# The softmax scaling of batch 0 moves from VectorE to GpSimd, ahead of the clearing of buffers

## The chip, the core and the metric

The kernel runs on one core of one Trainium2 chip. The metric is the time of one execution on the device in microseconds (us); lower is better. All numbers below are in us unless marked ns. TensorE multiplies matrices, VectorE (DVE in the rows) and ScalarE (ACT) do elementwise work, GpSimd (POOL) does elementwise work and issues its own DMAs, SyncE (SP) issues DMAs.

## What is computed

One layer on x of shape (8, 512, 512): 8 batches of 512 tokens with 512 features, all in float32.

```
xn  = layernorm(x)
out = x + attention(xn) + mixture_of_experts(xn)

attention, for each batch, 16 heads of 32, one key/value head for all:
    s = q @ k.T                 # 512 x 512, causal: row i sees columns 0..i
    p = exp(s - max) / sum      # softmax over each row
    o = p @ v
mixture of experts: 32 experts, 8 picked per token out of 2 of 4 groups,
    and a shared two-layer part (512 -> 1024 -> 512) with relu squared
```

## The kernel before, in words

The program has three parts, each written out engine by engine and held together by semaphores alone. `front` (0 to about 115 us) does the layer norm and the first projections. `middle` (about 115 to 1080 us) runs the 8 batches. `experts` does the routed experts to the end. The change lies in the first batch of `middle` (batch 0, about 115 to 260 us).

**A slot.** `middle` goes through each batch in 18 slots; slot s works on head s and finishes head s - 1. On TensorE a slot is: scores of head s for the row blocks 3 and 2, the down projection of the shared part for slot s - 2, scores of blocks 1 and 0, the first transposes of head s - 1, in slots 5, 9, 13 and 17 the product with the values, the up projection `up` of slot s (12 matmuls), more transposes of head s - 1, in slots 0, 4 and 8 the query projection of the next four heads, and the last transposes. The causal mask makes a head's four row blocks 512, 384, 256 and 128 columns wide, 1280 columns in all.

**VectorE's part of a slot.** `mask_and_min(s, i)` (L1088, a custom instruction that reads the scores from PSUM and the mask from SBUF) for two blocks; `shared(s - 1)`: two tensor_tensor instructions of 256 columns, L1104 and L1108, whose inputs both lie in SBUF; `mask_and_min` for two more blocks; in batch 0 a piece of the routing of the experts (it picks experts for all tokens); at last `scale(s)`: a reciprocal of the row sums (L1094) and four tensor_scalar instructions (L1098) that multiply the four blocks of `m_sc` in place by it.

**The other engines.** ScalarE computes the exponentials (L934) between `mask_and_min` and the reciprocal, then, in its slot s, the relu of `up` (L968), and copies of the transposes. In batch 0 ScalarE also rounds the last 9 of 21 pieces of the weights (`high_piece`, L170), two in each of the slots 0 to 3 and one in slot 4, always behind the relu of that slot. GpSimd subtracts to get the low part of each piece (L244) as soon as its high part is there. Behind the last piece GpSimd fills `empty`, writes it over the tail of `slot_rows` in device memory (`clear_tail`, L418: 31 x 128 rows of 1156 bytes) and over the spare rows of `sums` (L841). Its next work, scattering token rows to their expert slots (L856), is paced by batch 1's exponentials.

**Buffers that bind the order.** `m_sc` holds two heads. `mask_and_min(s)` waits until head s - 2 is scaled, exponentiated and fully transposed. The first transposes of head h wait for its scaling and for a copy by ScalarE.

Of the kernel before, what the change touches and what calls it, by code (L numbers as in the profile page):

```python
# [5 lines left out]
F32 = mybir.dt.float32  # L6
# [3 lines left out]
ALU = mybir.AluOpType  # L10
# [4 lines left out]
P = 128  # L15
B, S, D = 8, 512, 512
T = B * S
TB = S // P
G = T // P
KC = D // P  # L20
NH, HD = 16, 32
# [18 lines left out]
BASE = 16  # L40
# [15 lines left out]
def at(i, per, n):  # L56

    return i * per + (BASE + n)
# [38 lines left out]
def front(nc, sems, x, consts, fc1g, xnt_hi, xnt_lo, xh, xlo, rows, cst, logits, spare, weights, load_bias):  # L97


    with ExitStack() as ctx:  # L100
# [36 lines left out]
        piece_hi_made, piece_lo_made = sem("f_piece_hi_made"), sem("f_piece_lo_made")  # L137

        def part(which, piece):

            name, n = piece
            return weights[name][which][:, n * PIECE:(n + 1) * PIECE]
# [57 lines left out]
        def act_program(act, steps):  # L200
# [37 lines left out]

            in_a_row(((0, root), (1, high), (2, latent), (1, high_pieces)), B, R, steps)

        def pool_program(pool):
            for k, piece in enumerate(PIECES):
                pool.wait_ge(piece_hi_made, k + 1)
                nc.gpsimd.tensor_tensor(part(3, piece), part(1, piece), part(2, piece).bitcast(F32), ALU.subtract).then_inc(piece_lo_made, 1)  # L244

        def pe_program(pe, steps):
            if steps == FRONT_STEPS:
# [26 lines left out]
        def dve_program(dve, steps):  # L274
# [50 lines left out]
            if steps == FRONT_STEPS:  # L325
# [4 lines left out]
        last = (B // R - 1, R - 1)  # L330
        ends = dict(halves=(lo_made, after(*last, KC, KC)), latents=(xl_made, after(*last, TB, TB)), logits=(lg_made, after(*last, TB, TB)),
                    consts=(cst_in, 16), pieces=piece_lo_made,
                    halves_saved=[(xnt_saved[u], stored(B // R - 1 - u, u)) for u in range(R)],
                    latents_saved=[(xl_saved[u], xl_stored(B // R - 1, u)) for u in range(R)])
        return sp_program, pool_program, act_program, dve_program, pe_program, high_piece, ends


SHIFT_BLOCK = 4
# [9 lines left out]
PIECES_A_SLOT = 2  # L348
PIECES_OF = [(sum(PIECES_A_GROUP[:n]), sum(PIECES_A_GROUP[:n + 1])) for n in range(B)]
# [293 lines left out]
SPC = [0, 128, 384, 768]  # L643
# [31 lines left out]
def middle(nc, sems, x, bproj, xnt_hi, xnt_lo, xh, xlo, rows, wq, wkv, wproj, wup, wdown, cst, slots_sb, pads_sb, empty, xs, sums, partial,  # L675
# [3 lines left out]
    with ExitStack() as ctx:  # L679
# [73 lines left out]
        all_sent, tables_saved = sem("m_all_sent"), sem("m_tables_saved")  # L753

        NQ = 3 * 16

        def stacked(b, c):

# [74 lines left out]
                                  (xh_in, 32 * (B - 1)), (xlo_in, 32 * (B - 1))):  # L833
                sp.wait_ge(landed, value)

        def pool_program(pool):

            pool.wait_ge(*early["consts"])
            routing.clear_tail(pool)
            for a in sums:  # L840
                pool.dma_start(a[T:T + SPARE, :], empty[:, 0:LAT]).then_inc(zeroed, 16)  # L841
            pool.wait_ge(routing.slots_made, 2)
            pool.wait_ge(routing.pads_made, 1)
            pool.wait_ge(routing.tagged_saved, 16)
            pool.wait_ge(routing.expert_saved, 64)
            pool.wait_ge(routing.tail_sent, 16)
            for sem_, value in early["latents_saved"]:
                pool.wait_ge(sem_, value)

            def load(g):  # L850
                pool.dma_start(row[g % 2][:, :], rows[g * P:(g + 1) * P, :]).then_inc(row_in[g % 2], 16)

            def scatter(g, k):
                pool.wait_ge(exp_done, BASE + NH * TB + (g * TOPK + k) * PACE // (2 * TOPK))
                pool.sem_inc(pool_passed, 1)
                pool.indirect_dma_start(out=xs, out_offset=bass.IndirectOffsetOnAxis(ap=slots_sb[:, g, k:k + 1], axis=0),  # L856
                                        in_=row[g % 2][:, :], in_offset=None).then_inc(sent[g % 2], 16)

            def fill(g):
                pool.indirect_dma_start(out=xs, out_offset=bass.IndirectOffsetOnAxis(ap=pads_sb[:, g:g + 1], axis=0),  # L860
                                        in_=empty[:, :], in_offset=None, bounds_check=SLOTS - 1,
                                        oob_is_err=False).then_inc(pads_sent, 16)

            load(0)
            for g in range(G):
                if g % 2 == 0:
                    for a in sums:
                        pool.dma_start(a[g * P:(g + 2) * P, :].rearrange("(g p) l -> p g l", p=P),
                                       empty[:, 0:LAT].unsqueeze(1).broadcast_to([P, 2, LAT])).then_inc(zeroed, 16)
                pool.wait_ge(row_in[g % 2], 16 * (g // 2 + 1))  # L870
                pool.sem_inc(pool_passed, 1)
                for k in range(TOPK):
                    scatter(g, k)
                    if k == TOPK // 2 - 1 and g + 1 < G:
                        if g >= 1:
                            pool.wait_ge(sent[(g + 1) % 2], 16 * TOPK * ((g + 1) // 2))
                        load(g + 1)
                fill(g)
            for u in range(2):
                pool.wait_ge(sent[u], 16 * TOPK * G // 2)  # L880
            pool.wait_ge(pads_sent, 16 * G)
            pool.wait_ge(zeroed, 16 * len(sums) * (1 + G // 2))
            pool.sem_inc(all_sent, 1)
# [138 lines left out]
        def dve_program(dve, last_logits):  # L1022
# [55 lines left out]
            def batch(b, first):  # L1078
                def mask_and_min(h, i):
                    k = h * TB + ROWS.index(i)  # L1080
                    dve.wait_ge(s_done, at(b, NH * TB, k + 1))
                    if i == ROWS[0]:
                        dve.wait_ge(t_done, at(b, 3 * NH, 3 * (h - 1)))
                        dve.wait_ge(exp_done, at(b, NH * TB, TB * (h - 1)))
                        dve.wait_ge(scaled, at(b, NH, h - 1))
                    n = (i + 1) * P
                    dve.sem_inc(dve_passed, 1)
                    nc.vector.tensor_tensor_reduce(out=sc[:, h % 2, SPC[i]:SPC[i] + n], in0=psS[k % 2][:, 0:n],  # L1088
                                                   in1=mask[:, S - n:S], scale=1.0, scalar=3.0e38, op0=ALU.add,
                                                   op1=ALU.min, accum_out=low[:, h % 2, i:i + 1]).then_inc(s_out, 1)  # L1090

                def scale(h):
                    dve.wait_ge(exp_done, at(b, NH * TB, TB * (h + 1)))
                    nc.vector.reciprocal(inv[:, h % 2, :], total[:, h % 2, :]).then_inc(inv_made, 1)  # L1094
                    dve.wait_ge(inv_made, at(b, NH, h + 1))
                    for i in range(TB):
                        cols = sc[:, h % 2, SPC[i]:SPC[i] + (i + 1) * P]
                        last = nc.vector.tensor_scalar(cols, cols, inv[:, h % 2, i:i + 1], None, ALU.mult)  # L1098
                    last.then_inc(scaled, 1)
# [105 lines left out]
        def pe_program(pe, last_multiply):  # L1205
# [52 lines left out]
            def batch(b, first):  # L1258
# [35 lines left out]

                def transposes(h, g):
                    if g == 0:
                        pe.wait_ge(scaled, at(b, NH, h + 1))
                        pe.wait_ge(ta_out, at(b, 2 * NH, 2 * h))
                        todo = [(0, 0, i) for i in range(4)]
                    elif g == 1:  # L1300
# [489 lines left out]
def build(nc, x, w_fc1_gate, gate_bias, wq, wkv, wproj, bproj, wup, wdown, w1, w2, wfc2, consts, out):  # L1790
# [10 lines left out]
    with ExitStack() as ctx:  # L1801
        cst = ctx.enter_context(nc.sbuf_tensor("cst", [P, NCONST], F32))
        sems = ctx.enter_context(ExitStack())
        with ExitStack() as inner:
# [22 lines left out]
            def load_bias(sp):  # L1827
                sp.dma_start(bia, gate_bias.partition_broadcast(P)).then_inc(bias_in, 16)

            *early, high_piece, front_ends = front(nc, sems, x, consts, w_fc1_gate, xnt_hi, xnt_lo, xh, xlo, rows, cst, logits,  # L1830
                  front_spare[:, :, :].rearrange("p c n -> p (c n)"), {n: (w, raw[n], *halves[n]) for n, w in named}, load_bias)
            attention = middle(nc, sems, x, bproj, xnt_hi, xnt_lo, xh, xlo, rows, halves["wq"], halves["wkv"], (proj_raw, proj_hi, proj_lo), halves["wup"], halves["wdown"],
                   cst, slots_sb, pads_sb, empty, slot_rows, sums, partial, logits, biased, picked, ot, bias_in, bia, experts_dram, shifts_dram, wproj, front_ends)
# [9 lines left out]
        @block.gpsimd  # L1843
        def _(pool):
            early[1](pool)
            attention[1](pool)
            late[1](pool)

        @block.scalar
# [65 lines left out]
```

## Time and profile before

| | |
|---|---|
| time, median of 3 runs | 1730.41 (1730.21 to 1731.7) |
| the profiled execution: its time, its span | 1730.02, 1728.2 |
| busy in the span: TensorE, VectorE, ScalarE, GpSimd | 1620.8, 1205.5, 1073.1, 821.0 |
| mean granted TensorE clock | 0.986 of full |

The span is what the profiler saw of the execution's instructions; 1.8 lie around it. Busy times of an engine are sums over its instructions, so an engine that waits in one stage and is full in another shows a mean that describes neither. The times of the rows below count from the start of the span.

### The profile page before, as it was taken

How to read it: one execution, taken by the hardware profiler on the slowest of the kernel's cores; microseconds unless marked ns; L12 is line 12 of the kernel's file. 1: busy time of each engine (PE TensorE's matmuls, PEld its weight loads, DVE VectorE, ACT ScalarE, POOL GpSimd, SP SyncE). 2: the span in 40 equal slices, each digit the busy share in tenths (PEclk: the TensorE clock that was granted, in tenths of full speed). 3: DMA queues.
4: the chain of work that ended last, by engine and by line, in shares of the span. 5: the costliest groups of instructions: out<-in, count | busy, mean ns of one | idle time of the engine just before them, and what ended most of it. 6: DMA issues, size and time to landing. Idle time of an engine off the chain costs nothing.

```text
span 1728.2 us, 40624 instructions
## 1 busy us (share of the span) xinstructions
PE 1620.8 (94%) x10811; PEld 1388.4 (80%) x10811; DVE 1205.5 (70%) x3669; ACT 1073.1 (62%) x2799; POOL 821.0 (48%) x669
## 2 busy tenths in 40 slices
PE   5887789999999999999999999899999999999999
PEld 5775667777777877777777777799999999999987
DVE  7779987777868777778687777355555555555567
ACT  3355565666757756757577577366666666666642
POOL 0213002434524524435344344277777877778760
PEclk9899899999999999999999999999999999999999
DMA  7953823434434334344344344599999999989794
GB/s 280 387 166 102 134 63 99 142 115 145 140 96 151 124 126 153 113 137 136 116 138 133 105 151 141 117 183 188 182 195 187 189 187 198 201 172 162 137 260 184
DMA packets 193091, 273.72 MB, mean 158 GB/s; under 512 B 37400, under 2 KB 133791, under 8 KB 190820
## 3 DMA queue, kind: packets, MB, share of 16 engines
q0 software_dynamic: 60352, 92.59, 24.8%
q1 hardware_dynamic: 77572, 113.01, 23.2%
q10 hardware_dynamic: 54944, 65.52, 12.8%
q8 instruction: 94, 1.54, 0.4%
q14 instruction: 129, 1.06, 0.2%
HBM read 121.83 MB, written 129.67 MB: 146 GB/s over the span
## 4 chain that ended last, share of the span: by engine, by line
PE 58%; DVE 18%; issue 10%; DMA 5%; POOL 4%; ACT 3%; DVEq 1%; SPq 1%; ACTq 0%; POOLq 0%
PE e_psH L1710 10%; PE e_psY L1721 10%; DVE m_sc L1088 5%; POOL sums L1675 4%; PE m_psO L1339 4%; PE m_psU L64 3%; PE m_psS L1292 3%; PE m_psT L1317 3%; PE m_psY L64 3%; PE m_psU L66 3%; PE m_psU L65 3%; DVE m_sc L1098 3%; PE m_psY L65 3%; PE m_psY L66 3%; PE e_psX L1695 3%
## 5 line engine op out<-in xcount | busy, mean ns | idle before, releaser
L1675 POOL DMA_INDIRECT sums<-e_y,e_where x287 | 445.9, 1554 | 153.4 <-issue 96.5
L856 POOL DMA_INDIRECT slot_rows<-m_row,slots x256 | 266.1, 1039 | 470.4 <-ACT m_sc L934 436.8
L934 ACT ACTIVATE m_sc<-m_sc,m_low 128x512 f32<-128x512 f32 (+3 forms) x512 | 283.7, 556 | 161.5 <-DVE m_low L1088 160.1
L1710 PE MATMUL e_psH<-e_xt,e_w_of 128*128 128x128 f32 x2296 | 305.1, 276 | 3.3 <-ACT e_xt L1570 3.3
L1721 PE MATMUL e_psY<-e_w,e_ht 128*128 x1148 | 295.7, 380 | 1.5 <-ACT e_ht L1581 1.5
L1088 DVE CUSTOM_DVE_ANT_0 m_sc<-m_psS,cst 128x512 f32<-128x512 f32 (+3 forms) x512 | 229.4, 485 | 83.1 <-PE m_psS L1292 82.5
L1710 PEld LDWEIGHTS e_psH<-e_xt,e_w_of 128*128 128x128 f32 x2296 | 280.5, 193 | 3.7 <-ACT e_xt L1570 3.5
L1576 ACT ACTIVATE e_w_of<-e_w 128x512 f32 x287 | 180.9, 630 | 118.1 <-issue 116.1
L1721 PEld LDWEIGHTS e_psY<-e_w,e_ht 128*128 128x128 f32 x1148 | 196.2, 191 | 17.2 <-issue 2.5
L1292 PE MATMUL m_psS<-m_ks,m_qs 96*128 96x256 f32 (+2 forms) x512 | 160.2, 372 | 52.1 <-DVE m_low L1088 45.1
L1631 DVE TENSOR_SCALAR e_where<-e_row,e_shifts 128x1 uint32<-128x1 uint32 x287 | 61.5, 214 | 196.5 <-DMA sums<-e_y,e_where 178.2
L1098 DVE TENSOR_SCALAR m_sc<-m_sc,m_inv 128x128 f32<-128x128 f32 (+3 forms) x512 | 173.0, 407 | 4.5
L1581 ACT ACTIVATE e_ht<-e_relu 128x256 f32<-128x256 f32 x287 | 119.6, 417 | 87.5 <-DVE e_relu L1618 86.2
L1292 PEld LDWEIGHTS m_psS<-m_ks,m_qs 96*128 96x128 f32 x512 | 88.3, 191 | 98.4 <-DVE m_low L1088 84.2
L1618 DVE TENSOR_SCALAR e_relu<-e_psH 128x256 f32<-128x256 f32 x287 | 121.7, 424 | 60.1 <-PE e_psH L1710 58.7
L1317 PE MATMUL m_psT<-cst,m_sc 128*128 128x128 f32 x1082 | 163.1, 277 | 0.2
L64 PE MATMUL m_psU<-xh,wup_lo 128*128 128x256 f32 x512 | 157.6, 308 | 0.0
L66 PE MATMUL m_psU<-xh,wup_hi 128*128 128x256 f32 x512 | 146.2, 286 | 0.0
L65 PE MATMUL m_psU<-xlo,wup_hi 128*128 128x256 f32 x512 | 146.1, 285 | 0.0
L1634 DVE TENSOR_SCALAR e_y<-e_psY,e_row 128x256 f32<-128x256 f32 x287 | 139.0, 484 | 1.9 <-issue 1.7
L1317 PEld LDWEIGHTS m_psT<-cst,m_sc 128*128 128x128 f32 x1082 | 126.8, 143 | 3.6 <-issue 2.2
L1695 PE MATMUL e_psX<-cst,e_row 128*128 128x128 f32 x574 | 109.6, 273 | 0.0
(233 smaller groups left out, 3228.2 us busy)
## 6 DMA issues: line engine op xcount, KB each, us to landing
e_row<-slot_rows ACTq DMA_DIRECT2D x287, 144.5 KB, 3.7
m_qs<-m_qhi SPq DMA_DIRECT2D x256, 64.0 KB
e_w<-in_w SPq DMA_DIRECT2D x256, 64.0 KB
f_xt<-in_x SPq DMA_DIRECT2D x8, 1024.0 KB, 11.4
m_qs<-m_qlo SPq DMA_DIRECT2D x128, 64.0 KB
m_res<-in_x SPq DMA_DIRECT2D x8, 1024.0 KB, 5.8
sums<-empty POOLq DMA_DIRECT2D x32, 256.0 KB
partial<-m_res ACTq DMA_DIRECT2D x16, 512.0 KB
```

The costliest lines, as they stand in the source:

```text
L64: pe.matmul(out, ll, rh, start=first, stop=False)
L65: pe.matmul(out, lh, rl, start=False, stop=False)
L66: return pe.matmul(out, lh, rh, start=False, stop=last)
L856: pool.indirect_dma_start(out=xs, out_offset=bass.IndirectOffsetOnAxis(ap=slots_sb[:, g, k:k + 1], axis=0), in_=row[g % 2][:, :], in_offse ...
L934: nc.scalar.activation(cols, cols, ACT.Exp, bias=low[:, h % 2, i:i + 1], scale=-1.0, accum_out=total[:, h % 2, i:i + 1]).then_inc(exp_done, 1)
L1088: nc.vector.tensor_tensor_reduce(out=sc[:, h % 2, SPC[i]:SPC[i] + n], in0=psS[k % 2][:, 0:n], in1=mask[:, S - n:S], scale=1.0, scalar=3.0e ...
L1098: last = nc.vector.tensor_scalar(cols, cols, inv[:, h % 2, i:i + 1], None, ALU.mult)
L1292: pe.matmul(psS[k % 2][:, 0:n], qs[:, (b * NH + h) % QR, i * P:(i + 1) * P], ks[:, 0:n], start=True, stop=True).then_inc(s_done, 1)
L1317: mm = pe.transpose((*psT, psO)[bank][:, to:to + P], sc[:, h % 2, SPC[i] + j * P:SPC[i] + (j + 1) * P], ident)
L1675: pool.indirect_dma_start(out=both_sums, out_offset=bass.IndirectOffsetOnAxis(ap=where[u % NY][:, 0:1], axis=0), in_=y[u % NY][:, :], in_o ...
L1710: mm = pe.matmul(psH[u % 2][:, k * P:(k + 1) * P], w1_of[u % 2][:, c * INTER + k * P:c * INTER + (k + 1) * P], xt[u % 2][:, c * P:(c + 1) ...
L1721: mm = pe.matmul(psY[u % 2][:, 0:LAT], ht[u % 2][:, c * P:(c + 1) * P], w_f[:, bass.ds(e * (2 * W) + (W + c * LAT), LAT)], start=(c == 0), ...
```

## The change

In batch 0 the four multiplications of each head are issued by GpSimd (`scale_first`) and signalled by a semaphore of their own, `scaled0`. VectorE returns from `scale` right behind the reciprocal. GpSimd's instruction has a second operation, a multiplication by 1.0. GpSimd's program is written by slots: first the low parts of the pieces that ScalarE rounds in that slot, then the scaling of that head. Clearing the tail and zeroing the spare rows of `sums` come behind head 15. Batches 1 to 7 are as before.

```
+        def low_piece(pool, k):
+            pool.wait_ge(piece_hi_made, k + 1)
+            nc.gpsimd.tensor_tensor(part(3, PIECES[k]), part(1, PIECES[k]), part(2, PIECES[k]).bitcast(F32),
+                                    ALU.subtract).then_inc(piece_lo_made, 1)
         def pool_program(pool):
-            for k, piece in enumerate(PIECES):
-                pool.wait_ge(piece_hi_made, k + 1)
-                nc.gpsimd.tensor_tensor(part(3, piece), part(1, piece), part(2, piece).bitcast(F32), ALU.subtract).then_inc(piece_lo_made, 1)
+            for k in range(PIECES_OF[-1][1]):
+                low_piece(pool, k)
...
+        def scaled_to(b, n):
+            return (scaled0, BASE + n) if b == 0 else (scaled, at(b - 1, NH, n))
...
-        def pool_program(pool):
+        def pool_program(pool, low_piece):
+            def scale_first(h):
+                pool.wait_ge(inv_made, at(0, NH, h + 1))
+                for i in range(TB):
+                    cols = sc[:, h % 2, SPC[i]:SPC[i] + (i + 1) * P]
+                    last = nc.gpsimd.tensor_scalar(cols, cols, inv[:, h % 2, i:i + 1], 1.0, ALU.mult, ALU.mult)
+                last.then_inc(scaled0, 1)
+
+            pool.sem_inc(scaled0, BASE)
+            for h in range(NH):
+                held = PIECES_OF[-1][1] + PIECES_A_SLOT * h
+                for k in range(held, min(held + PIECES_A_SLOT, len(PIECES))):
+                    low_piece(pool, k)
+                scale_first(h)
             pool.wait_ge(*early["consts"])
             routing.clear_tail(pool)
...
-                        dve.wait_ge(scaled, at(b, NH, h - 1))
+                        dve.wait_ge(*scaled_to(b, h - 1))
...
                     dve.wait_ge(inv_made, at(b, NH, h + 1))
+                    if first:
+                        return
                     for i in range(TB):
...
-                        pe.wait_ge(scaled, at(b, NH, h + 1))
+                        pe.wait_ge(*scaled_to(b, h + 1))
```

On VectorE, at the end of head 0 and the start of head 1, the order before was this (L1094 is the reciprocal, L1098 the scaling, L1088 `mask_and_min` of head 1, L1104 and L1108 the shared part):

```order
L1094 RECIPROCAL m_inv<-m_total 128x4
L1098 TENSOR_SCALAR m_sc<-m_sc,m_inv 128x128
L1098 TENSOR_SCALAR m_sc<-m_sc,m_inv 128x256
L1098 TENSOR_SCALAR m_sc<-m_sc,m_inv 128x384
L1098 TENSOR_SCALAR m_sc<-m_sc,m_inv 128x512
L1088 ISA m_sc,m_low<-m_psS,cst 128x512
L1088 ISA m_low 128x1
L1088 ISA m_sc,m_low<-m_psS,cst 128x384
L1088 ISA m_low 128x1
L1104 TENSOR_TENSOR m_sq<-m_relu 128x256
L1108 TENSOR_TENSOR m_sq_parts<-m_sq,m_sq_parts 128x256
```

In the changed kernel the same place on VectorE reads (its line numbers are some 22 higher):

```order
L1116 RECIPROCAL m_inv<-m_total 128x4
L1110 ISA m_sc,m_low<-m_psS,cst 128x512
L1110 ISA m_low 128x1
L1110 ISA m_sc,m_low<-m_psS,cst 128x384
L1110 ISA m_low 128x1
L1128 TENSOR_TENSOR m_sq<-m_relu 128x256
L1132 TENSOR_TENSOR m_sq_parts<-m_sq,m_sq_parts 128x256
```

The four multiplications are gone from VectorE, and head 1's masking follows the reciprocal. On GpSimd the pieces of slots 1 to 4 and what followed them stood in one row before, with no other work between them:

```order
L244 TENSOR_TENSOR wdown_lo<-wdown_raw,wdown_hi 128x512
L244 TENSOR_TENSOR wq_lo<-wq_raw,wq_hi 128x512
L244 TENSOR_TENSOR wdown_lo<-wdown_raw,wdown_hi 128x512
L414 MEMSET empty 128x289
L416 CAST empty<-cst 128x1
L418 DMA slot_rows<-empty 128x31x289
L841 DMA sums<-empty 128x256 x2
```

In the changed kernel the same pieces (those of slots 3 and 4) stand between scalings, one head's four after each slot's pieces (the waits are printed):

```order
L851 TENSOR_SCALAR m_sc<-m_sc,m_inv 128x512
L243 TENSOR_TENSOR wdown_lo<-wdown_raw,wdown_hi 128x512 [waits f_piece_hi_made]
L243 TENSOR_TENSOR wq_lo<-wq_raw,wq_hi 128x512 [waits f_piece_hi_made]
L851 TENSOR_SCALAR m_sc<-m_sc,m_inv 128x128 [waits m_inv_made]
L851 TENSOR_SCALAR m_sc<-m_sc,m_inv 128x256
L851 TENSOR_SCALAR m_sc<-m_sc,m_inv 128x384
L851 TENSOR_SCALAR m_sc<-m_sc,m_inv 128x512
L243 TENSOR_TENSOR wdown_lo<-wdown_raw,wdown_hi 128x512 [waits f_piece_hi_made]
L851 TENSOR_SCALAR m_sc<-m_sc,m_inv 128x128 [waits m_inv_made]
```

A head's scaling now waits on GpSimd for that slot's pieces, and the clearing (L414 to L841 before) has moved behind the last of 64 multiplications.

## Rows read from the trace of the kernel before

**Rows 1.** Stretches of batch 0, then batch 1; column heads first.
```profile
core 0: us, PE busy (x) PEld busy (x) DVE busy (x) ACT busy (x) POOL busy (x), PEclk, DMA share, GB/s
115.00:250.00 135.00, 103.64 (x617) 84.57 (x616) 126.23 (x466) 78.89 (x221) 16.75 (x14) 0.90 0.43 91
278.00:371.00 93.00, 89.25 (x618) 73.86 (x617) 72.89 (x252) 69.36 (x206) 43.90 (x47) 1.00 0.40 130
```

**Rows 2.** The same view for line 1094 alone, the reciprocal that ends each head.
```profile
122.00:251.00 129.00, 2.83 (x16) 0.89 0.42 86
278.50:371.00 92.50, 2.77 (x16) 1.00 0.40 130
```

**Rows 3.** The same view for line 1098 alone, the scaling on VectorE.
```profile
122.00:253.00 131.00, 25.82 (x64) 0.88 0.42 86
278.50:373.00 94.50, 20.91 (x64) 1.00 0.41 130
```

**Rows 4.** Who waited for whom, 120 to 240 us: total, times, longest.
```profile
PEld m_psS L1292 <- DVE m_low L1088: 29.7, 20, 4.6
```

**Rows 5.** Timeline of VectorE around the end of head 10: start, duration.
```profile
216.27 1.28 DVE L1098 TENSOR_SCALAR m_sc<-m_sc,m_inv 128x128 f32<-128x128 f32 x4
217.46 0.69 DVE L1059 TENSOR_TENSOR m_qlo<-m_q,m_qhi 128x512 fp32r<-128x512 f32 x1
218.06 0.69 DVE L1088 CUSTOM_DVE_ANT_0 m_sc<-m_psS,cst 128x512 f32<-128x512 f32 x1
219.15 0.43 DVE L1104 TENSOR_TENSOR m_sq<-m_relu 128x256 f32<-128x256 f32 x1
219.61 0.42 DVE L1108 TENSOR_TENSOR m_sq_parts<-m_sq,m_sq_parts 128x256 fp32r<-128x256 f32 x1
```

**Rows 6.** Timelines of GpSimd and VectorE where their work meets, slots 2 and 4.
```profile
142.07 1.30 POOL L244 TENSOR_TENSOR wdown_lo<-wdown_raw,wdown_hi 128x512 fp32r<-128x512 f32 x1 [7.48 <-ACT wdown_hi L170]
143.32 1.27 POOL L244 TENSOR_TENSOR wup_lo<-wup_raw,wup_hi 128x512 fp32r<-128x512 f32 x1
142.46 3.00 DVE L1098 TENSOR_SCALAR m_sc<-m_sc,m_inv 128x128 f32<-128x128 f32 x4
...
153.85 1.46 POOL L244 TENSOR_TENSOR wq_lo<-wq_raw,wq_hi 128x512 fp32r<-128x512 f32 x1
154.20 1.40 DVE L1108 TENSOR_TENSOR m_sq_parts<-m_sq,m_sq_parts 128x256 fp32r<-128x256 f32 x1
```

**Rows 7.** Timeline of GpSimd: its instructions with two, no and one input.
```profile
54.27 1.26 POOL L244 TENSOR_TENSOR wkv_lo<-wkv_raw,wkv_hi 128x512 fp32r<-128x512 f32 x1 [53.82 <-ACT wkv_hi L170]
160.82 0.33 POOL L414 MEMSET empty<- 128x289 f32 x1
161.22 0.18 POOL L416 CAST empty<-cst 128x1 uint32<-128x1 f32 x1
```

**Rows 8.** Timelines of GpSimd, TensorE, ScalarE, VectorE, batch 0, heads 0 to 5.
```profile
123.07 1.26 POOL L244 TENSOR_TENSOR wup_lo<-wup_raw,wup_hi 128x512 fp32r<-128x512 f32 x1
137.12 1.05 PE L1317 MATMUL m_psT<-cst,m_sc 128*128 128x128 f32 x4
141.38 0.61 ACT L170 ACTIVATE wdown_hi<-wdown_raw 128x512 fp32r<-128x512 f32 x1
154.10 0.60 PE L1317 MATMUL m_psT<-cst,m_sc 128*128 128x128 f32 x4
160.85 0.65 PE L1292 MATMUL m_psS<-m_ks,m_qs 96*128 96x512 f32 x2
163.98 0.67 DVE L1088 CUSTOM_DVE_ANT_0 m_sc<-m_psS,cst 128x512 f32<-128x512 f32 x1
```

**Rows 9.** The cleared tail: its issue, its landing; TensorE behind batch 0.
```profile
161.72 2.11 POOL L418 DMA_DIRECT2D slot_rows<-empty  x1 [0.32 <-POOL empty L416]
...
slot_rows<-empty POOLq DMA_DIRECT2D x1, 4479.5 KB, 19.8
...
260.80 0.47 PE L64 MATMUL m_psS<-xh,wq_lo 128*128 128x512 f32 x1 [1.48 <-DMA xlo<-xnt_lo]
```

More of the change, by code:

```diff
@@ L334, in front @@
                     latents_saved=[(xl_saved[u], xl_stored(B // R - 1, u)) for u in range(R)])
-        return sp_program, pool_program, act_program, dve_program, pe_program, high_piece, ends
+        return sp_program, pool_program, act_program, dve_program, pe_program, high_piece, low_piece, ends
 SHIFT_BLOCK = 4
@@ L755, in middle @@
         NQ = 3 * 16
+        scaled0 = sem("m_scaled0")
+        def scaled_to(b, n):
+            return (scaled0, BASE + n) if b == 0 else (scaled, at(b - 1, NH, n))
         def stacked(b, c):
@@ L1828, in load_bias @@
                 sp.dma_start(bia, gate_bias.partition_broadcast(P)).then_inc(bias_in, 16)
-            *early, high_piece, front_ends = front(nc, sems, x, consts, w_fc1_gate, xnt_hi, xnt_lo, xh, xlo, rows, cst, logits,
+            *early, high_piece, low_piece, front_ends = front(nc, sems, x, consts, w_fc1_gate, xnt_hi, xnt_lo, xh, xlo, rows, cst, logits,
                   front_spare[:, :, :].rearrange("p c n -> p (c n)"), {n: (w, raw[n], *halves[n]) for n, w in named}, load_bias)
@@ L1845, in _ @@
             early[1](pool)
-            attention[1](pool)
+            attention[1](pool, low_piece)
             late[1](pool)
```

## The prediction, made before the changed kernel ran

> **What bounds the kernel now.** I first read the busy time by stretch and looked for where batch 0 differs from a later batch. In 135 us of batch 0 VectorE is busy 126.2 and TensorE 103.6; in 93 us of batch 1 TensorE is busy 89.3 and VectorE 72.9 [rows 1]. From the first head's reciprocal to the last one's, 15 heads on, batch 0 takes some 129 us and batch 1 some 92.5 [rows 2]. Batch 0 is paced by VectorE, which carries the routing beside its usual work, and the later batches by TensorE. The waits say the same from the other side: in batch 0 TensorE's loads of the scores' weights waited 29.7 for VectorE's masking [rows 4]. What is saved in batch 0 reaches the end, since every batch after it is queued behind it on TensorE. VectorE spent 25.8 on 64 scaling instructions in batch 0, against 20.9 for the same 64 in batch 1 [rows 3]; the 4.9 on top is where they met GpSimd's work (below).
>
> **What GpSimd's scaling costs.** The trace has no tensor_scalar on GpSimd, so its price X for one head (four instructions, 1280 columns) has to be bounded. A one-column cast took 0.18, which I take as the fixed part, 0.72 for four. A subtraction with two inputs and 512 columns took 1.26 [rows 7], so (1.26 - 0.18) / 512 = 2.11 ns for each column, and X is at most 0.72 + 2.70 = 3.4. A memset with no input took 0.33 for 289 columns, (0.33 - 0.18) / 289 = 0.52 ns, and X is at least 0.72 + 0.66 = 1.4. The scaling reads one tensor where the subtraction reads two. I take half of the subtraction's price for a column, 1.05 ns, and X = 0.72 + 1.35 = 2.1. The second operation of the instruction may add to that; I have no row for it and leave it to the upper bound.
>
> **What VectorE gains in a slot.** The block of four scalings stood 1.19 before the next instruction (217.46 - 216.27) [rows 5]. Taken out, masking follows the reciprocal. But now GpSimd works on the same head just then. What such a meeting does stands in the trace: beside a GpSimd subtraction that began at 153.85, VectorE's L1108, which has two inputs in SBUF, took 1.40 [rows 6] in place of 0.42 [rows 5]; and the four scalings took 3.00 beside two subtractions [rows 6] in place of 1.28 [rows 5]. An instruction of this kind waited out the other engine's instruction. After the change the two maskings (1.09 from 218.06 to 219.15 [rows 5], with the mask alone in SBUF) should pass, and L1104 and L1108 come behind them. With X = 2.1 GpSimd's instructions last 0.32, 0.45, 0.59 and 0.72 and start some 0.3 after the reciprocal, so that L1104 finds the third under way (0.4 to wait) and L1108 the fourth (0.7). That is 1.1 of the 1.19 given back in each slot in which VectorE sets the pace. In slots where VectorE waits for TensorE before masking, the two don't meet.
>
> The Trainium skill (SBUF — State Buffer, Who interferes with whom) says that a VectorE instruction with two SBUF inputs and a GpSimd instruction that reads SBUF exclude each other for the whole instruction. The 1.40 row agrees. By this rule a slot is worth 0.1; if the engines only shared bandwidth it would be worth near 1.2, and the whole change 5 more.
>
> **The ring in slots 0 to 4.** This is the term I expect to decide. GpSimd must do the low parts of slot h before it scales head h. Those wait for ScalarE's high parts, which stand behind the relu of `up(h)`; `up(h)` stands on TensorE behind the first transposes of head h - 1; and these now wait for GpSimd's scaling of head h - 1. So the scaling of one head hangs on that of the head before through three engines. Before, this was no ring, since VectorE did the scaling. Its length without scaling: head 1's transposes began at 137.12 and the second piece of slot 2 ended at 143.32 + 1.27 = 144.59, 7.5 later, with ScalarE's first high part at 141.38 in between [rows 6, 8]. With X and two handovers of 0.1 each it is 7.5 + 2.1 + 0.2 = 9.8. The granted clock of TensorE was 0.90 in this stretch against 1.00 in batch 1 [rows 1]; I leave the 7.5 as it is.
>
> The ring starts when slot 0's pieces end at 123.07 + 1.26 = 124.3 [rows 8]: scaling of head 0 ends at 124.3 + 2.1 + 0.4 (a meeting with VectorE) = 126.8, transposes of head 1 begin at 126.8 + 9.8 + 0.1 = 136.7 (before 137.12), of head 2 at 146.5, of head 3 at 156.3, where before it was 154.10: 2.2 late. The scores of head 5 follow these by 160.85 - 154.10 = 6.75 [rows 8], at 163.1, and VectorE masks them at 163.4. Before, it came to them at 163.98 only, though they stood ready from 161.5 (160.85 + 0.65) [rows 8]. So VectorE's saving in five heads, which could have been 1.19 x 5 + 4.9 = 10.9, shrinks to **+0.6**.
>
> **Heads 5 to 15.** I count slots 5, 6, 7, 11 and 12 as paced by VectorE (their routing work leaves no idle time in front of the reciprocal): 5 x (1.19 - 1.1) = **+0.5**. In 8 to 10 and 13 to 15 VectorE already waits for TensorE at times; there the saving reaches TensorE only as earlier scores. Between 0 and 6 x 1.19 = 7.1 I take **+1.5**, near the lower end, because TensorE's transposes now wait for a scaling that ends X + 0.3 behind the reciprocal and not 1.2.
>
> **The moved clearing.** GpSimd issued it at 161.72 in 2.11, and 4479.5 KB landed after 19.8 [rows 9]. Under slots 5 to 7 nothing waited for it. It moves behind head 15's scaling, with the two stores of `sums`, ahead of GpSimd's first scatters. There it lies beside SyncE's load of batch 1's second half and the stacking of its queries, and TensorE already waited 1.48 for that load at 260.80 [rows 9]. What is behind it on GpSimd, the scatters, is paced by batch 1's exponentials and spread over seven batches, so that 20 late costs nothing. The load is sent before the clearing's packets begin; the stacked queries are sent in the middle of them. Between 0 and 3 (a share of the 19.8 that a 64 KB move could lose) I take **-1.0**. What it frees in slot 4, where it held VectorE, is in the 4.9 above.
>
> **Sum.** 0.6 + 0.5 + 1.5 - 1.0 = 1.6 faster: the profiled execution's 1730.0 goes to 1728.4, and the median, 0.4 above it, to **1728.8**. A measurement of this kernel can tell about 0.2% (3.5 us) from no change, so this is no change. Its own range, 1725 to 1733, is X from 1.8 to 2.6: each 0.1 of X costs 0.4 in the ring and 0.3 to 0.6 in the five locked slots.
>
> **Rivals.**
> *Scaling is cheap on GpSimd.* With X = 1.4 the ring is 9.1 and stays within VectorE's own pace, and the four instructions (0.25 to 0.47) are nearly over before L1104: 1.0 a slot is kept. 0.6 + 2.8 + 5.0 + 1.5 - 1.0 = 8.9, so 1721. For it: one input, and the memset's rate. Against: the subtraction's rate is four times the memset's, and there are two operations. The skill's GPSIMD Engine Reference, Engine selection, calls one-input work on GpSimd roughly line-rate, which would be an estimate of X near 1.8; no row here shows it. 18%.
> *It works as meant.* No ring, no lock: VectorE loses 25.8 of work; six slots paced by TensorE keep 7 of it. 19 faster, 1711. For it: VectorE's 94% in batch 0. Against: the 1.40 and 3.00 rows, and the queue order on GpSimd. 8%.
> *The ring sets the pace, slower.* One mechanism: slots 0 to 4 run at 7.5 + X + 0.2. The gain of 1.6 is gone from X = 2.3 on. At X = 3.4 the ring is 11.1, its end 4 x 1.3 = 5.2 later, and the same X lengthens the locks by 0.7 in five slots and TensorE's wait for scaling by 1 in all: 0.6 - 5.2 - 3.5 - 1.0 - 1.0 = 10 slower, 1740. Range 1733 to 1746. For it: two operations and software on GpSimd. Against: nothing in the trace but the one input. 32%.
> The forecast has 42%.
>
> **Chances.** Faster by over 0.2% (below 1727): 18 + 8 + 12 of the forecast's 42 = 38%. Within 0.2%: 28%. Slower (above 1733.9): 32 + 2 = 34%. The range reaches from inside the cheap case to the upper bound of X: 1718 to 1741, with some 9% out on either side.
>
> **What would show it.** In the changed profile GpSimd's 64 multiplications give X at once. The ring is right if the pieces of slots 1 to 4 on GpSimd are some 9.8 apart and TensorE waits for GpSimd in front of its transposes. The lock is right if L1104 and L1108's counterparts (L1128, L1132) in slots 5 to 7 take over 0.42. The reciprocals of heads 0, 5 and 15, 129 us from first to last before [rows 2], split the ring from what follows. The clearing is right if batch 1's first scores start no more than 3 later against batch 0's last reciprocal. The prediction is wrong if X is outside 1.8 to 2.6, or if TensorE, less often idle, is granted a full clock throughout batch 0: that would shorten the ring.

## The result: 0.3% slower, and the profile after

The changed kernel took 1736.09 us (median of 8 runs, 1732.4 to 1741.9), the kernel before 1730.34 beside it (8 runs, 1727.59 to 1734.22): 1.0031 of its time, 95% interval 1.002 to 1.0042, or 5.75 us slower by the medians. The ratios here and below are computed from the fast runs and not from the two medians, and differ from the medians' quotient by up to 0.0006. The profiled execution took 1737.02 with a span of 1735.2. The first lines of its page, with the busy time of each engine:

```profile
span 1735.2 us, 40635 instructions
## 1 busy us (share of the span) xinstructions
PE 1624.7 (94%) x10811; PEld 1389.9 (80%) x10811; DVE 1190.2 (69%) x3605; ACT 1073.8 (62%) x2799; POOL 864.6 (50%) x733
```

VectorE was relieved (1205.5 to 1190.2) and GpSimd loaded (821.0 to 864.6), as the diff says. The stretch of batch 0 that [rows 1] show, in the changed kernel:

```profile
core 0: us, PE busy (x) PEld busy (x) DVE busy (x) ACT busy (x) POOL busy (x), PEclk, DMA share, GB/s
115.00:250.00 135.00, 104.57 (x607) 84.54 (x607) 107.38 (x399) 77.43 (x217) 49.87 (x68) 0.86 0.28 53
```

VectorE fell from 126.2 to 107.4 in the same 135 us, and yet TensorE did no more work in them (607 instructions for 617) and was granted less clock, 0.86 for 0.90. VectorE is no longer the bound here, and something else is. The reciprocals split where the time went. All are us behind head 0's reciprocal, from the profiled executions:

```
              head 5    head 15   first of batch 1
before         50.08    128.77    156.55
after          53.52    131.72    162.20
```

So heads 0 to 5 lost 3.4, heads 5 to 15 won 0.5, and the stretch behind head 15 lost 2.7: 5.6 in all, near the 5.75 of the medians. That the two agree so well is partly luck, for the spans of the two profiled executions differ by 7.0. The changed one stood 1.2 earlier at head 0's reciprocal and took 2.6 more behind batch 1's first one (1452.2 for 1449.6), where the change touches nothing but when GpSimd's first stores start. The same remainder is 1451.3 to 1459.1 in the profiles of the experiments below, so nothing ties it to one part of the change.

**The ring.** GpSimd's timeline for slots 0 to 4 of the changed kernel (the row of a scaling is its block of four; in brackets how long the engine stood idle, and for whom):

```profile
121.92 1.27 POOL L243 TENSOR_TENSOR wup_lo<-wup_raw,wup_hi 128x512 fp32r<-128x512 f32 x1
123.17 2.81 POOL L851 TENSOR_SCALAR m_sc<-m_sc,m_inv 128x128 f32<-128x128 f32 x4
131.09 1.29 POOL L243 TENSOR_TENSOR wdown_lo<-wdown_raw,wdown_hi 128x512 fp32r<-128x512 f32 x1 [5.11 <-ACT wdown_hi L170]
132.34 1.45 POOL L243 TENSOR_TENSOR wup_lo<-wup_raw,wup_hi 128x512 fp32r<-128x512 f32 x1
133.77 3.61 POOL L851 TENSOR_SCALAR m_sc<-m_sc,m_inv 128x128 f32<-128x128 f32 x4
142.58 1.29 POOL L243 TENSOR_TENSOR wdown_lo<-wdown_raw,wdown_hi 128x512 fp32r<-128x512 f32 x1 [5.21 <-ACT wdown_hi L170]
143.82 1.73 POOL L243 TENSOR_TENSOR wup_lo<-wup_raw,wup_hi 128x512 fp32r<-128x512 f32 x1
145.53 2.55 POOL L851 TENSOR_SCALAR m_sc<-m_sc,m_inv 128x128 f32<-128x128 f32 x4
...
152.94 1.45 POOL L243 TENSOR_TENSOR wq_lo<-wq_raw,wq_hi 128x512 fp32r<-128x512 f32 x1
154.37 3.09 POOL L851 TENSOR_SCALAR m_sc<-m_sc,m_inv 128x128 f32<-128x128 f32 x4
...
163.91 2.06 POOL L851 TENSOR_SCALAR m_sc<-m_sc,m_inv 128x128 f32<-128x128 f32 x4
```

The first idle of each slot ends with ScalarE's high part, never with a reciprocal; the scaling follows the pieces without a gap. On TensorE the same slots show the other side, the first transposes of heads 0 to 3, and the scores of head 5:

```profile
126.04 1.12 PE L1341 MATMUL m_psT<-cst,m_sc 128*128 128x128 f32 x4 [3.03 <-POOL m_sc L851]
...
137.43 1.12 PE L1341 MATMUL m_psT<-cst,m_sc 128*128 128x128 f32 x4 [4.96 <-POOL m_sc L851]
...
148.13 0.66 PE L1341 MATMUL m_psT<-cst,m_sc 128*128 128x128 f32 x4 [2.19 <-POOL m_sc L851]
...
157.51 1.12 PE L1341 MATMUL m_psT<-cst,m_sc 128*128 128x128 f32 x4 [4.61 <-POOL m_sc L851]
...
165.56 0.65 PE L1316 MATMUL m_psS<-m_ks,m_qs 96*128 96x512 f32 x2
```

The turns are 11.4, 10.7 and 9.4 long. Four transposes took 1.12 behind the waits of 3.0, 5.0 and 4.6, and 0.66 behind the one of 2.2. VectorE in slots 3 and 5 of the same kernel:

```profile
152.37 0.90 DVE L1128 TENSOR_TENSOR m_sq<-m_relu 128x256 f32<-128x256 f32 x1
153.30 1.38 DVE L1132 TENSOR_TENSOR m_sq_parts<-m_sq,m_sq_parts 128x256 fp32r<-128x256 f32 x1
...
166.21 0.69 DVE L1110 CUSTOM_DVE_ANT_0 m_sc<-m_psS,cst 128x512 f32<-128x512 f32 x1 [5.24 <-PE m_psS L1316]
...
167.76 0.42 DVE L1132 TENSOR_TENSOR m_sq_parts<-m_sq,m_sq_parts 128x256 fp32r<-128x256 f32 x1
```

VectorE, once the bound, stood idle 5.24 for head 5's scores; before, they waited for it. The waits of 120 to 250 us, in total, number and longest. TensorE's wait for the masking, the last of them, was 32.6 in this window before (29.7 up to 240 us, [rows 4]):

```profile
PEld m_psT L1341 <- POOL m_sc L851: 18.2, 8, 5.2
DVE m_sc L1110 <- PE m_psS L1316: 17.2, 8, 5.2
...
PEld m_psS L1316 <- DVE m_low L1110: 14.9, 17, 4.1
```

**The clearing.** GpSimd behind head 15's scaling, which answers to [rows 9]:

```profile
257.10 2.00 POOL L422 DMA_DIRECT2D slot_rows<-empty  x1 [0.32 <-POOL empty L420]
259.11 1.15 POOL L863 DMA_DIRECT2D sums<-empty  x2
275.74 0.54 POOL L873 DMA_DIRECT2D m_row<-rows  x1 [15.48 <-DMA slot_rows<-empty]
```

and TensorE at batch 1's first scores, with the granted clock in the stretch that begins there and in an equal one behind it:

```profile
276.29 1.12 PE L1316 MATMUL m_psS<-m_ks,m_qs 96*128 96x512 f32 x2 [3.02 <-DMA m_qs<-m_qlo]
```

```profile
276.20:279.70 3.50, 3.41 (x9) 2.78 (x10) 1.18 (x4) 1.41 (x4) 1.54 (x3) 0.52 0.98 321
280.00:283.40 3.40, 3.40 (x23) 3.07 (x22) 1.57 (x7) 1.35 (x6) 2.06 (x2) 1.00 0.43 154
```

TensorE waited 3.02 for the stacked queries, which SyncE had sent while the clearing's packets were under way (the low parts at 270.84; the clearing, issued at 257.10, landed 17.9 later), and then worked for 3.4 us at half clock (1.2 GHz).

### The profile page after: what moved, and what is told of

Same layout as the page of the kernel before. It is cut to its first block, busy times and chain, and to the rows that moved or that the text cites. A ratio compares the mean times of both kernels' runs of the same rounds, so it can differ in the third digit from the quotient of the medians.

```text
span 1735.2 us, 40635 instructions
## 1 busy us (share of the span) xinstructions
PE 1624.7 (94%) x10811; PEld 1389.9 (80%) x10811; DVE 1190.2 (69%) x3605; ACT 1073.8 (62%) x2799; POOL 864.6 (50%) x733
## 3 DMA queue, kind: packets, MB, share of 16 engines
q14 instruction: 128, 1.05, 0.2%
## 4 chain that ended last, share of the span: by engine, by line
PE 67%; DVE 15%; issue 7%; DMA 4%; ACT 4%; POOL 2%; SPq 1%; DVEq 1%; ACTq 0%; POOLq 0%
PE e_psH L1734 14%; PE e_psY L1745 14%; DVE m_sc L1110 5%; PE m_psO L1363 4%; PE m_psU L64 4%; PE m_psT L1341 4%; PE e_psX L1719 4%; PE m_psU L66 3%; PE m_psU L65 3%; PE m_psS L1316 3%; PE m_psY L64 3%; PE m_psY L65 3%; PE m_psY L66 3%; DVE m_sc L1122 2%; ACT m_sc L956 2%
## 5 line engine op out<-in xcount | busy, mean ns | idle before, releaser
L1122 DVE TENSOR_SCALAR m_sc<-m_sc,m_inv 128x128 f32<-128x128 f32 x448 | 147.3, 399 | 4.0
```

## The experiments

Each was timed against the kernel before on its own chip (1730.48, 1730.45 and 1731.52 there). "Head 5" and so on are the marks of the table above. A mark is read from one execution, which can lie 3 us or more from the median of its kernel. So a mark tells where a time goes, and the median how much it is. Two pairs of profiles show how far a mark scatters. Up to head 5 the first experiment has the program of the changed kernel, and head 5 stood at 52.2 in it and at 53.5 there. The second has that of the kernel before, with 48.9 and 50.1.

**The clearing, alone.** From the changed kernel, the clearing goes back early, behind head 4's scaling:

```
                 scale_first(h)
+                if h == 4:
+                    pool.wait_ge(*early["consts"])
+                    routing.clear_tail(pool)
+                    for a in sums:
+                        pool.dma_start(a[T:T + SPARE, :], empty[:, 0:LAT]).then_inc(zeroed, 16)
-            pool.wait_ge(*early["consts"])
-            routing.clear_tail(pool)
-            for a in sums:
-                pool.dma_start(a[T:T + SPARE, :], empty[:, 0:LAT]).then_inc(zeroed, 16)
```

> The changed kernel with one part undone: GpSimd clears the tail and zeroes the spare rows behind head 4's scaling, about where it did before, and not behind head 15's. Theory 'the late clearing delays the stacked queries': batch 1's first scores no longer wait (3.0 us) for the DMA of the stacked queries, the stretch from head 15's reciprocal to the first one of batch 1 falls from 30.5 to about 27.8 us, and the time from about 1736 to about 1733.3. Rival 'the stretch is longer for another reason (ScalarE or TensorE behind it, a granted clock at half)': it stays near 30.5 and the time near 1736.

It took 1733.15 (1.0018, 1.0001 to 1.0034), 2.7 above the kernel before where the changed kernel is 5.75 above it; the intervals of the two overlap, and it is the mark that shows the place. Head 15 to batch 1's first reciprocal was 26.6, where the changed kernel has 30.5; the wait for the stacked queries was gone, and the clock there stayed at 1.00. The opposite, late clearing in the kernel before, with nothing else changed:

```
             pool.wait_ge(*early["consts"])
+            pool.wait_ge(t_done, at(0, 3 * NH, 3 * (NH - 1) + 1))
             routing.clear_tail(pool)
```

> The kernel before with one part of the change alone: VectorE scales as ever, but GpSimd's clearing waits for the first transposes of head 15. Theory 'the late clearing delays the stacked queries': heads 0 to 15 as before (128.8 us from first to last reciprocal), the stretch behind them 30 to 31 us in place of 27.8, the time about 1733. Rival 'the clearing is free there': 27.8 and 1730.4. With the scaling on VectorE the heads 0 to 15 tell nothing of it in either theory.

It took 1737.25 (1.0045, 1.0025 to 1.0064), 4 more than expected and no less than the changed kernel itself. The last stretch went from 27.8 to 32.3, and TensorE waited in it like this, in that kernel's trace:

```profile
272.50 1.12 PE L1293 MATMUL m_psS<-m_ks,m_qs 96*128 96x512 f32 x2 [4.25 <-DMA m_qs<-m_qlo]
```

So moving the clearing costs 3.9 and 4.5 us by the marks, 3.1 and 6.8 by the medians, scaling on GpSimd or not. In all six profiles with the late clearing TensorE waited for the stacked queries (3.0 to 4.3), and the 3.5 us behind the wait ran at 0.50 to 0.61 of the clock. In none of the others did it wait for them.

**The ring, cut.** In the changed kernel each head is scaled first, and the pieces of its slot come behind it:

```
             for h in range(NH):
+                scale_first(h)
                 held = PIECES_OF[-1][1] + PIECES_A_SLOT * h
                 for k in range(held, min(held + PIECES_A_SLOT, len(PIECES))):
                     low_piece(pool, k)
-                scale_first(h)
```

> The changed kernel, but in each slot GpSimd scales the head first and makes the low parts of the slot's pieces behind it. Theory 'ring': the scaling of head h no longer hangs on the up projection of its own slot; TensorE's waits for GpSimd in front of the transposes (16 us in batch 0) fall below 5, the first five heads fall from 53.5 us to 50 or less, and the time from about 1736 to 1730 to 1732. Rival 'lock only': what costs is VectorE and GpSimd meeting, which goes on; the five heads stay at 52 to 54 us and the time at 1735 or more.

It took 1731.58 (1.0004, 0.9992 to 1.0016), no longer slower than the kernel before, though the clearing is still late in it. Head 5's reciprocal stood at 46.6, 7.0 earlier than in the changed kernel and 3.5 earlier than before. Two lines changed places, and the first half of batch 0 went from a loss to a gain. The other way to leave the ring is to leave heads 0 to 4 to VectorE:

```
-                scale_first(h)
+                if h >= 5:
+                    scale_first(h)
...
-                    if first:
+                    if first and (h >= 5):
                         return
...
-                    last.then_inc(scaled, 1)
+                    last.then_inc(scaled0 if first else scaled, 1)
```

> The changed kernel, but VectorE still scales heads 0 to 4 and GpSimd heads 5 to 15; the clearing stays behind head 15. Theory 'ring plus lock': the first five heads take 50.1 us as in the kernel before; from head 5 to head 15 it takes 78 us, as in the changed kernel (78.2) and hardly less than before (78.7), since the lock and the later transposes eat the 1.2 us a slot; with 2.7 lost in the clearing the time is 1732 to 1733. Rival 'from head 5 on the move works as meant and only the ring spoils it': 70 to 73 us from head 5 to 15 and a time of 1725 to 1727.

It took 1733.08 (1.0009, 0.9995 to 1.0022): head 5 at 50.2 as before, heads 5 to 15 in 75.7 (before 78.7), the last stretch 30.7. With the early clearing as well:

> VectorE scales heads 0 to 4, GpSimd heads 5 to 15, and GpSimd clears the tail behind the last piece, about where it did before. No ring and no late clearing: the sum of what e1 and e4 showed. First five heads 50.2 us, heads 5 to 15 76 us, the stretch behind them 26.7 to 27.8: batch 1 starts 153 to 154 us behind head 0's reciprocal (156.6 before), and the time is 1727 to 1728. Rival 'the clearing in slot 5 costs what it did not cost at the end': 156 or more and 1730.

1728.73 (0.9989, 0.9974 to 1.0004), the last stretch 26.6. Heads 5 to 15 took 78.1 in this profile, though but for the clearing the program there is that of the 75.7. Most of the difference is in one slot, head 14's. It took 10.8 in four profiles (the changed kernel and the experiments so far with the clearing early, the pieces behind, and this one), and in all four TensorE's clock was 0.62 or 0.63 from 3 us before head 13's reciprocal to 1 behind it. In the profile of the 75.7, and in the three below that scale all heads with two operations and no extra work, it was 1.00, and the slot took 9.2 to 9.7. A gain of 0.5 or of 3 in this stretch thus comes with the clock of one execution and not with the program. Up to head 13 the scatter is small: heads 5 to 13 took 64.5 before and 61.9 to 63.3 in all these versions.

**Both repairs.** Pieces behind the scaling, clearing behind head 4:

> All 16 heads on GpSimd, each slot's pieces behind its scaling, the clearing behind head 4's scaling. The sum of what e1 and e3 showed: first five heads 46.6 us, heads 5 to 15 77.3, the stretch behind them 26.7 to 27.8; batch 1 starts 150.6 to 151.7 us behind head 0's reciprocal against 156.6 before, and the time is 1724.5 to 1726. Rival 'batch 0 is bound elsewhere, and what is saved in the first heads is given back': 154 or more and a time within 2 us of before.

1724.85 (0.9971, 0.9959 to 0.9984): faster than both kernels, 5.6 less than before. Its marks are 46.2, 121.9 and 148.3. That profiled execution took 1721.96, the lowest of its 12 runs, so the marks promise more than the median gives. The first scalings and first transposes, in its trace:

```profile
120.83 2.22 POOL L851 TENSOR_SCALAR m_sc<-m_sc,m_inv 128x128 f32<-128x128 f32 x4 [22.93 <-DVE m_inv L1117]
...
130.86 2.21 POOL L851 TENSOR_SCALAR m_sc<-m_sc,m_inv 128x128 f32<-128x128 f32 x4 [4.71 <-DVE m_inv L1117]
```

```profile
133.13 0.66 PE L1342 MATMUL m_psT<-cst,m_sc 128*128 128x128 f32 x4 [0.54 <-POOL m_sc L851]
...
142.62 0.66 PE L1342 MATMUL m_psT<-cst,m_sc 128*128 128x128 f32 x4 [0.53 <-POOL m_sc L851]
```

The scaling waits for the reciprocal now, and TensorE for the scaling only 0.54. Of all waits of this kernel from 119 to 255 us these two carry the comparison with the 18.2 and 14.9 above:

```profile
PEld m_psS L1317 <- DVE m_low L1111: 23.3, 22, 5.5
PEld m_psT L1342 <- POOL m_sc L851: 8.6, 11, 1.6
```

VectorE sets the pace again, with less to do.

**Is it a ring? More work in it.** Four small multiplications ahead of each head's scaling on GpSimd, into a buffer that nothing reads, once in the changed kernel and once in the version with both repairs:

```
+                for n in range(0, 16, 4):
+                    nc.gpsimd.tensor_scalar(spare_cols[:, h % 2, n:n + 4], mask[:, n:n + 4],
+                                            inv[:, h % 2, 0:1], 1.0, ALU.mult, ALU.mult)
```

> The changed kernel with four small GpSimd multiplications (4 columns, into a tile of their own that nobody reads) in front of each head's scaling, some 0.2 us each, 0.8 a head. Theory 'ring': in slots 0 to 4 GpSimd's time is on the path once a slot, so that the first five heads grow from 53.5 by four times 0.8, to about 56.7 us, and the time by 3 us or more, to 1739 to 1742. Rival 'GpSimd's length does not set the first heads' pace': 53 to 54.5 us there.

> The same four small multiplications in e7, where the pieces stand behind the scaling and there is no ring. Theory 'ring': 0.8 more a head is mostly hidden in the first five heads (46.2 to at most 47.5 us), and the time is 1725 to 1728. Rival: if GpSimd's length is on the path without the pieces in front as well, the first five heads grow by 3 us, as in e11.

They cost about 1.3 a head (64 of them 21.1 us) and not the 0.8 expected. In the changed kernel it took 1744.79 (1.0077, 1.0058 to 1.0095): the first transposes of heads 0 to 3 were 13.5, 11.8 and 12.0 apart, 5.8 more in three turns, and head 5 stood 6.3 later. With both repairs it took 1730.04 (0.999, 0.9977 to 1.0003), head 5 2.1 later. The same work costs three times as much in heads 0 to 5 where the pieces stand ahead of it. It is not free in the other version either, where both marks and time are above what was expected: TensorE waits up to 2.2 there for the scaling in place of 0.54. Over the whole kernel the work costs 7.5 us in the first and 4.1 in the second, by the medians against the kernel before beside each.

**The lock.** VectorE's two instructions with two SBUF inputs (L1128, L1132) come behind the last two maskings of their slot in batch 0:

```
-                    if 1 <= s <= NH:
+                    if 1 <= s <= NH and not first:
                         shared(s - 1)
...
                         mask_and_min(s, ROWS[3])
+                    if 1 <= s <= NH and first:
+                        shared(s - 1)
```

> The changed kernel, but in batch 0 VectorE does all four maskings before the two instructions of the shared part (L1128, L1132), so that they come some 0.7 us later, when GpSimd's scaling is mostly over. Theory 'lock': their busy time in batch 0, 19.4 us in the changed kernel against 14.5 before, falls toward 14; if the lock sets the pace in the slots with much routing, heads 5 to 15 fall from 78.2 to 76 us or less and the time by 2 to 3 us, to about 1733. Rival 'the lock is paid where VectorE has time': the busy time falls but heads 5 to 15 stay at 77.5 to 78.5 and the time stays at 1736; the first five heads may move either way, since the other instructions with two inputs still meet GpSimd's pieces.

1738.68 (1.0051, 1.0035 to 1.0067), no faster than the changed kernel. First how long the two were in the changed kernel, batch 0 and then batch 1, where GpSimd doesn't scale (the columns are the stretch, its length, VectorE's busy time in L1128 alone, the granted clock, the DMA share and GB/s; the second fence is the same for L1132):

```profile
119.00:256.00 137.00, 8.88 (x16) 0.85 0.26 49
278.00:375.00 97.00, 6.28 (x15) 0.99 0.41 136
```

```profile
119.00:256.00 137.00, 10.50 (x16) 0.85 0.26 49
278.00:375.00 97.00, 6.37 (x15) 0.99 0.41 136
```

Free they are 6.7 and 6.8 for 16, so meetings cost 2.2 + 3.7 = 5.9, or 0.37 a slot. In the kernel before they took 14.5 together in batch 0, so 4.9 of the 19.4 came with the change. In the experiment they took 7.61 and 7.59, so 4.2 was taken away, and still head 5 stood at 53.4 as in the changed kernel. Heads 5 to 15 took 75.7, as the theory of the lock had it, but 1.2 of those 2.5 are head 14's slot at full clock, and the last stretch took 32.8 for 30.5. Why the first heads won nothing is seen in slot 1, on GpSimd and on VectorE:

```profile
134.35 4.29 POOL L851 TENSOR_SCALAR m_sc<-m_sc,m_inv 128x128 f32<-128x128 f32 x4
```

```profile
135.80 0.77 DVE L1068 TENSOR_TENSOR m_q<-m_q,m_rot 128x512 f32<-128x512 f32 x1
136.49 0.68 DVE L488 TENSOR_TENSOR ot<-proj_raw 128x512 f32<-128x512 f32 x1
137.09 0.98 DVE L489 TENSOR_TENSOR ot<-proj_raw 128x512 f32<-128x512 f32 x1
```

The scaling met L1128 and L1132 at its start (134.01 to 135.16) and then the two-input instructions of the rotation and the routing, and took 4.29. In the changed kernel it had met the rotation and the routing too, and took 3.61. The same edit on the version with both repairs:

> e7 with the later shared part of e5. If the lock matters, 1 to 3 us less than e7 (1722 to 1725), heads 5 to 15 in 75 to 76 us; if it is paid where VectorE has time, the same as e7 within 1 us.

1726.66 (0.998, 0.9967 to 0.9992), 1.8 more than without it, with intervals that overlap; batch 1's first reciprocal stood 2.4 later. The 1 to 3 us that the lock should have given did not come.

**The second operation.** In the version with both repairs, one operation in place of two:

```
-                    last = nc.gpsimd.tensor_scalar(cols, cols, inv[:, h % 2, i:i + 1], 1.0, ALU.mult, ALU.mult)
+                    last = nc.gpsimd.tensor_scalar(cols, cols, inv[:, h % 2, i:i + 1], None, ALU.mult)
```

> e7 with one operation in GpSimd's multiplication in place of two (no second multiplication by 1.0). If the second operation costs nothing, the block of four undisturbed stays at 2.06 us and the time at 1725; if it costs what the step from one operation to two could, the block falls below 1.9 and the time by up to 1 us.

1738.4 (1.0041, 1.0027 to 1.0054), 13.6 more than with two, or 12.5 when each is taken against the kernel before on its own chip. The narrowest and the widest instruction of a block that met nothing, first with one operation and then with two (the block at 163.91 of the changed kernel):

```profile
161.73 0.60 POOL L851 TENSOR_SCALAR m_sc<-m_sc,m_inv 128x128 f32<-128x128 f32 x1 [3.28 <-DVE m_inv L1117]
...
164.45 1.56 POOL L851 TENSOR_SCALAR m_sc<-m_sc,m_inv 128x512 f32<-128x512 f32 x1
```

```profile
163.91 0.37 POOL L851 TENSOR_SCALAR m_sc<-m_sc,m_inv 128x128 f32<-128x128 f32 x1
...
165.28 0.70 POOL L851 TENSOR_SCALAR m_sc<-m_sc,m_inv 128x512 f32<-128x512 f32 x1
```

Such a block of four took 4.26 to 4.28 against 2.06. The multiplication by 1.0 is what makes the scaling affordable on GpSimd at all.

## Why the prediction was wrong, point by point

The forecast was no change (1728.8). The time came out 5.75 slower, above the forecast's own range of 1725 to 1733 and inside the outer one of 1718 to 1741. It lies in the rival "the ring sets the pace", whose mechanism it was, but not at that rival's price: that one needed X above 2.3. (Its sum for X = 3.4 also leaves out the +0.5 and +1.5 of heads 5 to 15; with them it is 8 slower and not 10.)

**X = 2.1: right, partly by luck, and used wrongly.** A block that met nothing took 2.06. Its instructions took 0.37, 0.48, 0.59 and 0.70, which is 0.26 and 0.86 ns a column, where the prediction had 0.18 and 1.05: one part too low and the other too high. And only one of the five blocks in slots 0 to 4 met nothing; together they took 2.81 + 3.61 + 2.55 + 3.09 + 2.06 = 14.1, or 2.8 each. The prediction had the rows that say so: [rows 6] show that an instruction waits out the other engine's. It charged that to VectorE alone, and to GpSimd only once, 0.4 for head 0. It also looked at L1104 and L1108 alone. What stood beside the block of 3.61 (133.77 to 137.38) was VectorE's rotation and routing, which have two inputs in SBUF as well:

```profile
134.55 0.75 DVE L1066 TENSOR_TENSOR m_rot<-m_rot,cst 128x512 f32<-128x512 f32 x1
135.34 0.95 DVE L1068 TENSOR_TENSOR m_q<-m_q,m_rot 128x512 f32<-128x512 f32 x1
136.22 0.68 DVE L488 TENSOR_TENSOR ot<-proj_raw 128x512 f32<-128x512 f32 x1
```

The block's last two instructions took 1.02 and 1.64 beside them, 0.59 and 0.70 when alone. The Trainium skill (SBUF — State Buffer, Who interferes with whom) says the same for both sides: whoever begins first holds the port pair, and the other blocks. The trace agrees, with 1.38 for L1132 behind the subtraction of 152.94, and with 3.61 and 4.29 for the blocks beside the rotation and the routing.

**The ring, +0.6 predicted, -3.4 measured: the step that failed.** The place, the order and the carrier were right; the turn was mis-sized. Predicted were three turns of 9.8, measured 11.4, 10.7 and 9.4, 2.1 more in all. The blocks in them took 9.25 in place of 6.3, which alone is 3.0; what is left of a turn was 0.3 shorter each than the 7.5 + 0.2. The start was 0.4 later against head 0's reciprocal (125.98 - 120.84 = 5.14 for 4.78), so head 3's transposes were 2.4 behind the forecast (36.7 for 34.3 behind head 0's reciprocal). From them to the scores of head 5 it took 8.05 and not 6.75 [rows 8], 1.3 more. TensorE had stood idle 4.6 and then worked without a pause, but at 0.63 of the clock, where it had 1.00 for this piece before; the two windows, changed and before:

```profile
157.50:165.56 8.06, 8.05 (x34) 7.21 (x35) 3.33 (x20) 2.40 (x5) 2.90 (x5) 0.63 0.00 1
154.10:160.85 6.75, 5.44 (x35) 4.65 (x35) 6.54 (x23) 4.00 (x13) 3.30 (x3) 1.00 0.45 155
```

That and 0.3 at VectorE make 4.0, the whole difference. "I leave the 7.5 as it is" held for the turns, but the ring makes TensorE wait, and behind three of the four waits above it ran at half clock: the last piece of the way had to be priced at the lower level. That the turn is a ring and not a sum of delays is shown by the reordering, which won 7.0 at head 5, and by the two experiments with extra work (6.3 against 2.1). How much of the loss is the lock and how much the clock was worked out from the rows of one profile, not separated by an experiment; the same program showed head 5 at 52.2 in another, a loss of 2.1.

**The lock, 1.1 a slot predicted, 0.37 measured on VectorE.** The 0.37 is the mean of 16 slots. In the five slots that the term was for (5, 6, 7, 11 and 12), L1128 and L1132 exceeded 0.42 by 0, 0.47, 0.43, 0 and 0.41 together, 0.26 in the mean. The mechanism was right, the term four times too large. GpSimd lost more on its side, which the term didn't have: 16 blocks took 42.1, 2.6 each against 2.06. And moving the two won nothing that can be told from noise.

**Heads 5 to 15, +2.0 predicted, +0.5 measured, 3.0 in three other profiles.** Right as far as can be told. Up to head 13 the changed kernel won 1.7; head 14's slot cost 1.9 (10.8 for 8.9) and the next gave 0.7 back. The clock around head 13's reciprocal goes with the difference between 0.5 and 3, and why it falls in some executions was not settled.

**The moved clearing, -1.0 predicted, -2.7 in the profile and -3.9 to -6.1 by the experiments: the second term that failed.** The last stretch of the changed kernel, 30.5, is 3.9 above the same kernel with the early clearing; the pair with the pieces behind differs by 6.1 (32.5 and 26.5), the pair from head 5 on by 4.1, the kernel before by 4.5. By medians the pairs differ by 3 to 7. The -2.7 against the kernel before is 3.9 less 1.2 for what else was shorter there, TensorE's 1.48 for the load of `xlo` [rows 9] above all. That wait is in no other profile but the last experiment's (0.66), the kernel before with the late clearing included, so it seems to belong to one execution and not to the change. The prediction had the place ("the stacked queries are sent in the middle of them"), and the wait itself, 3.02, is at its bound of 3; the whole cost is beyond it. It missed what follows the wait: 3.5 us at 0.52 of the clock, which do about half the work, so 1.7 more. It also took a value near the low end, though the very transfer that batch 1 begins with lay in the 19.8 of the clearing.

**The sum.** -3.4 + 0.5 - 2.7 = -5.6 against +1.6. The gain was there as well: with both repairs the kernel is 5.6 faster than before by the medians.

## What to carry to other kernels

When work moves to another engine, ask what already stands ahead of it in that engine's queue and what this is itself waiting for: if the answer leads back to the moved work, the price of one turn counts once for every slot, and putting the short urgent work ahead of the slow patient work can turn the loss into a gain. Price a meeting of two engines for both of them, against all that each does in that slot, and a wait of several us on TensorE with the clock that the rows show behind such a wait. A bulk transfer that nobody waits for isn't free to move: what counts is which small transfer it lies beside.

## What the runs showed of the hardware that was not expected

**One operation cost twice what two do on GpSimd.** With float32 and a column of numbers as the scalar, an instruction of 128x512 elements that met nothing took 1.56 with one operation and 0.70 with two (means over all 16, meetings included, 1568 and 823 ns). The slope between 128 and 512 columns is (1.56 - 0.60) / 384 = 2.5 ns a column with one, and (0.70 - 0.37) / 384 = 0.86 with two. The Trainium skill (GPSIMD Engine Reference, Elementwise — side-by-side cycle accounting) gives 1.03 cycles an element for the shortest loop bodies, which at its 1.2 GHz is an estimate of 0.86 ns. The form with two operations agrees with it; the form with one is three times slower, and no run here shows why.

**The fixed part of a small instruction is not 0.18.** A multiplication of 128x4 took 0.26 where it met nothing (0.35 and 0.33 in the mean of 64 each), and the straight line through the widths of the scaling gives 0.26 at no columns. The prediction took its fixed part from a one-column cast of 0.18.
